# State space loop: five of ScalarE's bank reads for the linear attention taken one unit later

## The chip, the cores and the metric

The kernel runs on one core of a Trainium2 chip. The metric is the device time of one execution in microseconds. The time before is 1586.47 us, the median of three runs (1583.47 to 1590.08).

## What is computed

A decoder of two layers over 8 sequences of 256 tokens, 256 features, fp32. Layer 0 is an attention, a cross attention and a mixture of experts; layer 1 is a state space layer, a linear cross attention and a second mixture of experts. A layer norm stands behind each. The change touches the stretch in which the state space layer and the linear attention run together:

```python
# state space layer, h: 256 features x 16 states
h = exp(delta_t * A) * h + (delta_t * x_t) * B_t ;  y_t = sum_n h * C_t   # for every t
y = ys + D * x
# linear attention, context c, 16 heads of 16
K = c @ Wk.T + bk ; V = c @ Wv.T + bv ; Q = x @ Wq.T + bq
context = einsum('bhld,bhle->bhde', softmax(K, axis=tokens), V)
out = einsum('bhld,bhde->bhle', Q, context) @ Wo.T + bo
```

The context of a sequence does not depend on x. So the kernel computes for each sequence b, ahead of time, one matrix `w2[b] = Wq-part @ masked context @ Wo` and one row `lbias[b]`, and later only `x @ w2[b] + lbias[b]`.

## The kernel before

`state_space_and_linear_layers` handles the 2048 tokens in 4 chunks of 512 (two sequences each). A unit is one of the 16 states in one chunk, so there are 64 units, u = 0 to 63, with c = u // 16 and n = u % 16. Each engine runs its own loop over the units:

- VectorE (`block.vector`): in unit u, `inputs(u + 1)` (L2231, dx times the row of B in a PSUM bank), now and then a piece of the time steps (L2213, `biased`) or the attended rows (L2250, `attended`), then two scans (L2345), one for each half of the features. Each scan waits for its decay.
- ScalarE (`block.scalar`): in unit u, `decays(u + 1, 0)`, `row_of_b(u + 2)` (L2087), `decays(u + 1, 1)` (L2081), then the tasks of the unit. A decay of half h (of 128) waits until scan h - 3 is done (three banks), so `decays(u + 1, 1)` waits for the first scan of unit u. `row_of_b(u + 2)` waits until `inputs(u + 1)` is done, as there is one bank for the row.
- POOL: `h * C` (L2010) when both scans are done. TensorE: `accumulate(u - 2)` (L2410), which adds these products in PSUM, then its jobs of unit u.

The jobs are TensorE's pieces of work that go through two PSUM banks by turns (`j_banks`). The list `JOBS` numbers them: for each unit first the work for the next chunk (`AHEAD_JOBS`: T0, T1, R, D0, D1 at n = 1 to 5), then that for the chunk before (`BEHIND_JOBS`: Y0, Y1, X0, X1, Z0, Z1 at n = 2, 3, 8 to 11), then that of the linear attention (`LINEAR_JOBS`, by u % 7, a sequence every 7 units). On TensorE `start(name)` waits until the job two places before has been read out of its bank, by VectorE for D and Z, by ScalarE for all others. ScalarE reads the jobs in this order, and `j_act` counts its reads, so a waiter asks for `COUNT[name]`.

The jobs of the linear attention and ScalarE's instructions for them (`linear(job, b)` in the ScalarE block):

- u % 7 = 0: Lc (context of the sequence before, L2135) and LcT (context rows transposed, L2124)
- 1: Lk, keys: two instructions (L2127)
- 2: LM, masked context times Wo (L2138)
- 3: Lv, values (L2130), and behind it `exponentials` of the keys (L2147)
- 4: LW, combined weights (L2140)
- 5: Lb, bias row (L2142), and behind it `softmax` (L2153)
- 6: LkR, keys transposed back (L2132)

VectorE takes the maxima of the keys (L2358) at the end of its unit 7b + 2, behind the scans; it waits for ScalarE's read of Lk. The softplus (L2063, L2065) is at n = 6, the normalisations of y and z (L2092) at n = 7 and 14; TensorE's transposes X0 wait for the first.

Of the kernel before, what the change touches and what calls it, by code (L numbers as in the profile page):

```python
# [1766 lines left out]
def state_space_and_linear_layers(nc, block, sems, used_sems, x, arrivals, early, S, w, ctx_in, lw):  # L1767
# [28 lines left out]
    with ctx:  # L1796
# [66 lines left out]

        SEQS, ND = T // S, S // 128
        LINEAR_JOBS = {0: (("Lc", 1), ("LcT", 0)), 1: (("Lk", 0),), 2: (("LM", 1),), 3: (("Lv", 0),), 4: (("LW", 1),), 5: (("Lb", 1),), 6: (("LkR", 0),)}
        assert PERIOD * (SEQS + 1) < UNITS

        def linear_jobs_at(u):

            return [(job, u // PERIOD - behind) for job, behind in LINEAR_JOBS[u % PERIOD] if 0 <= u // PERIOD - behind < SEQS]  # L1870

        def sequence_at(u, n):

            return u // PERIOD if u % PERIOD == n and u // PERIOD < SEQS else None
# [165 lines left out]
        def _(act):  # L2040
# [3 lines left out]
            def taken(name):  # L2044

                act.wait_ge(j_raw, NUMBER[name] + 1)
                return bank_of(name)

            def columns(c, half):
                b = taken(f"T{half}.{c}")  # L2050
                at = c % 2 * W + half * 256
                nc.scalar.copy(xT[:, :, at:at + 256].rearrange("p k (t s) -> p t k s", t=2),
                               b.rearrange("p (t k s) -> p t k s", t=2, k=KD)).then_inc(j_act, 1)

            def projected(c):
                b = taken(f"R.{c}")
                if c >= 2:
                    act.wait_ge(bc_stored, 32 * (c - 1))
                nc.scalar.copy(rbc[:, cols(c)], b).then_inc(j_act, 1)

            def softplus(c):
                act.wait_ge(j_dve, COUNT[f"D1.{c}"])
                nc.scalar.activation(delta[:, :, cols(c)], delta[:, :, cols(c)], ACT.Exp).then_inc(dt_exp, 1)  # L2063
                act.wait_ge(dt_exp, c + 2)
                nc.scalar.activation(delta[:, :, cols(c)], delta[:, :, cols(c)], ACT.Ln, bias=one[:, 0:1]).then_inc(dt_soft, 1)  # L2065
# [7 lines left out]
            def decays(u, k):  # L2073
                c, n, half = u // N, u % N, 2 * u + k
                if u == 0:
                    act.wait_ge(dt_first, k + 1)
                elif half == 2 * N * c:
                    act.wait_ge(dt_ready, c)
                if half >= 3:
                    act.wait_ge(scanned, half - 2)  # L2080
                nc.scalar.activation(after_first(decay_ps[half % 3][:]), after_first(delta[:, k, cols(c)]), ACT.Exp,  # L2081
                                     scale=neg_a[:, k, n:n + 1]).then_inc(decayed, 1)

            def row_of_b(u):
                act.wait_ge(bc_in[u % BC_RING], 16 * (u // BC_RING) + 16)
                act.wait_ge(inp_ready, u + 1)
                nc.scalar.copy(b_ps[:], bc_rows[:, u % BC_RING, 0, :]).then_inc(b_copied, 1)  # L2087

            def normalise(c, z):
                act.wait_ge(s_shift[z], c + 1)  # L2090
                for t in range(TC):
                    last = nc.scalar.activation(x[:, c * TC + t, :], x[:, c * TC + t, :], ACT.Identity, bias=shift[z][:, t:t + 1], scale=rstd[z][:, t:t + 1])  # L2092
                last.then_inc(s_norm[z], 1)

            def normalise_arrived(n):
                act.wait_ge(m_shift, n - ON_POOL + 1)
                for t in range(arrived_parts[n].start, arrived_parts[n].stop):
                    last = nc.scalar.activation(x[:, t, :], x[:, t, :], ACT.Identity, bias=shift_m[:, t:t + 1], scale=rstd_m[:, t:t + 1])
                last.then_inc(m_norm, 1)
# [5 lines left out]
            def behind(c, job):  # L2105
                if job[0] == "Y":
                    rows_back(c, int(job[1]))
                elif job[0] == "X":
                    columns_again(c, int(job[1]))

            def total(c):
                act.wait_ge(y_total, c + 1)
                nc.scalar.copy(ysum[:, c % 2, :], y_ps[:]).then_inc(y_copied, 1)
# [6 lines left out]
            def linear(job, b):  # L2120
                p = taken(f"{job}.{b}")
                halves_of = p.rearrange("p (k s) -> p k s", k=KD)
                if job == "LcT":
                    nc.scalar.copy(cT[:], halves_of).then_inc(j_act, 1)  # L2124
                elif job == "Lk":
                    for m in range(KD):
                        last = nc.scalar.activation(kT[:, m, :], halves_of[:, m, :], ACT.Identity, bias=lbk[:, m:m + 1])  # L2127
                    last.then_inc(j_act, 1)
                elif job == "Lv":
                    nc.scalar.copy(lv[:], halves_of).then_inc(j_act, 1)  # L2130
                elif job == "LkR":
                    nc.scalar.copy(kR[:], halves_of).then_inc(j_act, 1)  # L2132
                elif job == "Lc":
                    for m in range(KD):
                        last = nc.scalar.activation(cmT[:, m, :], p[:, m * 128:m * 128 + 128], ACT.Identity, bias=lbv[:, m:m + 1])  # L2135
                    last.then_inc(j_act, 1)
                elif job == "LM":
                    nc.scalar.copy(cwo[:], halves_of).then_inc(j_act, 1)  # L2138
                elif job == "LW":
                    nc.scalar.copy(w2[:, b], halves_of).then_inc(j_act, 1)  # L2140
                else:
                    nc.scalar.copy(lbias[:, b, :], p[:, 0:D]).then_inc(j_act, 1)  # L2142

            def exponentials(b):
                act.wait_ge(k_maxed, b + 1)
                for m in range(KD):
                    last = nc.scalar.activation(kT[:, m, :], kT[:, m, :], ACT.Exp, bias=k_nmax[:, m:m + 1], accum_out=k_sums[:, m:m + 1])  # L2147
                last.then_inc(k_exped, 1)

            def softmax(b):  # L2150
                act.wait_ge(k_recip, b + 1)
                for m in range(KD):
                    last = nc.scalar.activation(kT[:, m, :], kT[:, m, :], ACT.Copy, scale=k_sums[:, m:m + 1])  # L2153
                last.then_inc(k_soft, 1)
# [14 lines left out]
            for u in range(UNITS):  # L2169
                c, n = u // N, u % N  # L2170
                if u + 1 < UNITS:
                    decays(u + 1, 0)
                    if u + 2 < UNITS:
                        row_of_b(u + 2)
                    decays(u + 1, 1)
                for m in range(ON_POOL, len(arrived_parts)):
                    if u == NORM_M_AT[m]:
                        normalise_arrived(m)
                if c + 1 < CH:
                    if n in AHEAD_JOBS and AHEAD_JOBS[n][0] == "T":  # L2180
                        columns(c + 1, int(AHEAD_JOBS[n][1]))
                    elif n in AHEAD_JOBS and AHEAD_JOBS[n] == "R":
                        projected(c + 1)
                    elif n == SOFT_AT:
                        softplus(c + 1)
                if c >= 1:
                    if n == EVAC_AT:
                        total(c - 1)
                    if n in BEHIND_JOBS:
                        behind(c - 1, BEHIND_JOBS[n])  # L2190
                    for z in "yz":
                        if n == NORM_AT[z]:
                            normalise(c - 1, z)
                for job, b in linear_jobs_at(u):
                    linear(job, b)
                if sequence_at(u, 3) is not None:
                    exponentials(sequence_at(u, 3))
                if sequence_at(u, 5) is not None:
                    softmax(sequence_at(u, 5))
# [423 lines left out]
```

## Time and profile before

| | |
|---|---|
| median of 3 runs | 1586.47 us (1583.47 to 1590.08) |
| profiled execution, its own time | 1588.36 us |
| its span, first to last instruction | 1586.6 us |
| mean granted TensorE clock | 0.933 |
| PE busy | 1384.8 us (87%) |
| VectorE (DVE) busy | 1104.2 us (70%) |
| ScalarE (ACT) busy | 934.5 us (59%) |
| POOL busy | 822.6 us (52%) |

The first scan of the loop starts at 1023.3 us and the last one ends near 1278 us. Ahead of it lie the attentions and the first mixture of experts, behind it the second one. Shares over the whole span say little about the loop. It is read from windows: the timeline of a stretch gives for each engine the start, the length, the line and, in brackets, the idle time before it and whose work ended that idle time.

### The profile page before, as it was taken

To read this page: it belongs to the slowest core of one execution; us is meant where nothing else is said; L and a number is where in the kernel's file an instruction comes from. 1 tells how busy PE (TensorE), PEld (TensorE's weight loads), DVE (VectorE), ACT (ScalarE), POOL (GpSimd) and SP (SyncE) were. 2 spreads that over 40 slices of the span, in tenths; PEclk is the share of its full clock that TensorE was granted. 3 is DMA by queue.
4 is the path that set the end of the run, shared out by engine and by line. 5 is a ranking of instruction groups with operands and counts; after the bars stand their busy time and mean duration, and the time that the engine had idled before them with its cause. 6 is when DMAs were issued, how large, how long until landed. Compare 5 with 4: busy or idle time off the path is not lost.

```text
span 1586.6 us, 27670 instructions
## 1 busy us (share of the span) xinstructions
PE 1384.8 (87%) x9268; PEld 1121.8 (71%) x9268; DVE 1104.2 (70%) x2434; ACT 934.5 (59%) x2307; POOL 822.6 (52%) x862
## 2 busy tenths in 40 slices
PE   4778999999999999956999999689899969898891
PEld 3556777777777777645999999345555549888781
DVE  5677776666666666557788874698999945656535
ACT  4666565555655655542688861377788725356553
POOL 3664554444444444433688861288868740255550
PEclk8899999999999999956999999899999987889996
DMA  4100000000000000047456668644343310244574
GB/s 150 37 28 7 28 8 8 2 8 3 6 8 2 7 2 1 1 147 272 174 202 229 233 204 298 238 133 147 124 146 135 133 60 21 94 159 162 191 250 175
DMA packets 52942, 167.85 MB, mean 106 GB/s; under 512 B 13178, under 2 KB 22340, under 8 KB 44996
## 3 DMA queue, kind: packets, MB, share of 16 engines
q1 hardware_dynamic: 45316, 145.63, 26.0%
q0 software_dynamic: 7488, 20.46, 4.0%
q8 instruction: 77, 1.26, 0.3%
q14 instruction: 61, 0.50, 0.1%
HBM read 149.28 MB, written 16.78 MB: 105 GB/s over the span
## 4 chain that ended last, share of the span: by engine, by line
PE 33%; DVE 8%; POOL 6%; issue 6%; ACT 3%; DMA 2%; POOLq 0%; DVEq 0%; ACTq 0%; SPq 0%
PE m_ps L1713 11%; PE m_ps L1736 10%; POOL s_hc L2010 4%; PE m_ps L1710 2%; DVE s_h L2345 2%; PE m_ps L1731 2%; PE m_ps L1693 1%; PE m_ps L1633 1%; PE s_yps L2410 1%; ACT s_dps L2081 1%; PE m_ps L1643 1%; PE s_yps L2497 1%; DVE tokens L1600 1%; PE m_ps L1661 1%; DMA arrived<-in_down 0%
## 5 line engine op out<-in xcount | busy, mean ns | idle before, releaser
L306 POOL TENSOR_TENSOR a_pexp<-a_pexp,a_rsum 128x384 f32<-128x384 f32 (+1 forms) x320 | 246.4, 788 | 302.6 <-DVE a_rsum L523 302.6
L396 ACT ACTIVATE a_pexp<-a_ps,a_nmax 128x384 f32<-128x384 f32 (+1 forms) x320 | 181.2, 566 | 171.7 <-DVE a_nmax L519 171.1
L1713 PE MATMUL m_ps<-m_xT,m_w1s 128*128 128x256 f32 x1344 | 213.0, 298 | 19.9 <-issue 15.3
L1736 PE MATMUL m_ps<-m_w2s,m_hs 128*128 128x256 f32 x1344 | 205.2, 290 | 4.9 <-issue 3.9
L1713 PEld LDWEIGHTS m_ps<-m_xT,m_w1s 128*128 128x128 f32 x1344 | 187.9, 203 | 23.4 <-issue 17.6
L519 DVE TENSOR_REDUCE a_nmax<-a_ps 128x1 f32<-128x384 f32 (+1 forms) x320 | 154.0, 523 | 71.1 <-PE a_ps L620 70.1
L1736 PEld LDWEIGHTS m_ps<-m_w2s,m_hs 128*128 128x128 f32 x1344 | 183.1, 197 | 6.8 <-issue 6.0
L2010 POOL TENSOR_TENSOR s_hc<-s_h,s_bc_rows 128x1024 f32<-128x1024 f32 x64 | 151.1, 2365 | 54.5 <-DVE s_h L2345 53.3
L1096 POOL DMA_INDIRECT m_xrow<-table,m_row_from x78 | 80.5, 1032 | 143.9 <-DVE m_row_from L1431 106.7
L2345 DVE TENSOR_TENSOR_SCAN s_h<-s_dps,s_inp 128x512 f32<-128x512 f32 x128 | 148.9, 1206 | 0.0
L636 PE MATMUL a_ps<-a_ident,a_pexp 128*128 128x128 f32 x896 | 144.2, 273 | 3.4 <-ACT a_pT L255 3.0
L2410 PE MATMUL s_yps<-s_hc,s_ident 128*128 128x512 f32 x256 | 124.9, 611 | 14.6 <-POOL s_hc L2010 14.2
L1113 POOL DMA_INDIRECT results<-m_yrow,m_row_to x78 | 83.5, 1071 | 75.2 <-ACT m_yrow L1225 58.8
L636 PEld LDWEIGHTS a_ps<-a_ident,a_pexp 128*128 128x128 f32 x896 | 107.3, 140 | 16.2 <-POOL a_pexp L306 5.1
L654 PE MATMUL a_ps<-a_pT,a_vx 128*64 128x256 f32 x768 | 97.0, 387 | 4.0 <-DVE a_qs_low L476 4.0
L2081 ACT ACTIVATE s_dps<-s_delta,neg_a 128x510 f32<-128x510 f32 x128 | 88.7, 693 | 12.9 <-DVE s_h L2345 12.4
L934 POOL TENSOR_TENSOR m_w2s<-arrived,m_w2s 128x512 fp32r<-128x512 f32 x60 | 79.0, 1318 | 26.6 <-ACT m_w2s L1161 26.0
L257 DVE COPY a_pT<-a_ps 128x384 f32<-128x384 f32 x128 | 70.1, 548 | 25.7 <-PE a_ps L636 25.7
L2410 PEld LDWEIGHTS s_yps<-s_hc,s_ident 128*128 128x128 f32 x256 | 47.1, 194 | 57.1 <-issue 32.7
L2231 DVE TENSOR_TENSOR s_inp<-s_dx,s_bps 128x1024 f32<-128x1024 f32 x63 | 75.9, 1204 | 11.7 <-ACT s_bps L2087 11.3
L1205 ACT ACTIVATE m_ps<-m_ps,m_b 128x256 f32<-128x256 f32 x128 | 58.4, 457 | 41.6 <-PE m_ps L1713 40.2
L1205 ACT ACTIVATE m_ps<-m_ps 128x256 f32<-128x256 f32 x96 | 35.6, 372 | 75.6 <-PE m_ps L1713 74.1
(402 smaller groups left out, 3432.4 us busy)
## 6 DMA issues: line engine op xcount, KB each, us to landing
s_bc_rows<-s_bc_table SPq DMA_DIRECT2D x64, 512.0 KB, 3.7
arrived<-in_down SPq DMA_DIRECT2D x29, 1024.0 KB, 6.5
arrived<-in_up SPq DMA_DIRECT2D x23, 1024.0 KB
m_w<-in_up SPq DMA_DIRECT2D x24, 512.0 KB
m_w<-in_down SPq DMA_DIRECT2D x24, 512.0 KB
arrived<-results SPq DMA_DIRECT2D x3, 1024.0 KB, 8.5
m_fin<-results SPq DMA_DIRECT2D x4, 768.0 KB
tokens<-in_x SPq DMA_DIRECT2D x8, 256.0 KB, 6.9
```

The costliest lines, as they stand in the source:

```text
L306: nc.gpsimd.tensor_tensor(pexp[:, r, 0:n], pexp[:, r, 0:n], rsum[:, r:r + 1].to_broadcast([128, n]), ALU.mult).then_inc(normed, 1)
L396: nc.scalar.activation(pexp[:, r, 0:n], ps_s[score_bank(u)][:, 0:n], ACT.Exp, bias=nmax[:, r:r + 1], accum_out=sums[:, r:r + 1]).then_inc( ...
L519: nc.vector.tensor_reduce(nmax[:, u % RING:u % RING + 1], ps_s[score_bank(u)][:, 0:keys_of(u)], AX.X, ALU.max, negate=True).then_inc(maxed, 1)
L636: last = nc.tensor.transpose(pt_bank(n)[:, at + k * 128:at + k * 128 + 128], pexp[:, g % RING, k * 128:k * 128 + 128], ident[:])
L654: last = nc.tensor.matmul(ps[BANK["pv", m]][64 * h:64 * h + 64, 0:S], vals[:, k, p * 128 + 64 * h:p * 128 + 64 * h + 64], pT[:, m % 2, h, ...
L1205: nc.scalar.activation(hid, hid, act, bias=b1[:, number % B_BUFS, ft:ft + 1] if b_up is not None else 0.0).then_inc(h_act, 1)
L1713: last = nc.tensor.matmul(ps_hid[ft % RING], w1s[wb][wp][:, k, of], xT[:, j % 2, xp, k, :], start=(k == 0 and wp == 0 and xp == 0), stop=( ...
L1736: last = nc.tensor.matmul(ps_y[j % 2][:, s, :], hs[hp][:, ft % RING, s * 128:(s + 1) * 128], w2s[wb][wp][:, ft, :], start=(ft == 0 and s = ...
L2010: nc.gpsimd.tensor_tensor(halves(hc[:, u % HC_RING, :]), halves(h[:, u % H_RING, :]), bc_rows[:, u % BC_RING, 1, :].unsqueeze(1).to_broadc ...
L2081: nc.scalar.activation(after_first(decay_ps[half % 3][:]), after_first(delta[:, k, cols(c)]), ACT.Exp, scale=neg_a[:, k, n:n + 1]).then_in ...
L2345: nc.vector.tensor_tensor_scan(h[:, u % H_RING, of], decay_ps[(2 * u + k) % 3][:], inp[:, u % I_RING, of], 0.0, ALU.mult, ALU.add).then_in ...
L2410: last = nc.tensor.matmul(y_ps[:, k * W:(k + 1) * W], ident[:], hc[:, u % HC_RING, k * W:(k + 1) * W], start=(n == 0), stop=False)
```

## The change

ScalarE reads the banks of five of the eight linear jobs (Lk, LM, Lv, LW, Lb) not at the end of its tasks of unit u but in unit u + 1, right behind the decays and the row of B. The order of its reads is kept, and TensorE issues all jobs where it did.

```diff
--- before.py
+++ after.py
@@ -1863,6 +1863,7 @@
 
         SEQS, ND = T // S, S // 128
         LINEAR_JOBS = {0: (("Lc", 1), ("LcT", 0)), 1: (("Lk", 0),), 2: (("LM", 1),), 3: (("Lv", 0),), 4: (("LW", 1),), 5: (("Lb", 1),), 6: (("LkR", 0),)}
+        LATE_JOBS = ("Lk", "LM", "Lv", "LW", "Lb")
         assert PERIOD * (SEQS + 1) < UNITS
 
         def linear_jobs_at(u):
@@ -2173,6 +2174,9 @@
                     if u + 2 < UNITS:
                         row_of_b(u + 2)
                     decays(u + 1, 1)
+                for job, b in linear_jobs_at(u - 1):
+                    if job in LATE_JOBS:
+                        linear(job, b)
                 for m in range(ON_POOL, len(arrived_parts)):
                     if u == NORM_M_AT[m]:
                         normalise_arrived(m)
@@ -2192,7 +2196,8 @@
                         if n == NORM_AT[z]:
                             normalise(c - 1, z)
                 for job, b in linear_jobs_at(u):
-                    linear(job, b)
+                    if job not in LATE_JOBS:
+                        linear(job, b)
                 if sequence_at(u, 3) is not None:
                     exponentials(sequence_at(u, 3))
                 if sequence_at(u, 5) is not None:
```

## Rows read from the trace of the kernel before

**Rows 1.** busy time by stretch: us, busy of each engine (x instructions), PEclk, DMA share, GB/s

```profile
1023.00:1279.00 256.00, 225.14 (x798) 136.55 (x799) 242.56 (x284) 196.76 (x379) 202.72 (x124) 0.97 0.40 134
...
1118.00:1143.00 25.00, 23.66 (x97) 16.05 (x96) 24.38 (x33) 21.28 (x43) 24.50 (x14) 1.00 0.39 129
...
1190.00:1206.00 16.00, 14.45 (x65) 10.41 (x66) 14.61 (x15) 11.63 (x23) 15.92 (x9) 1.00 0.40 136
1206.00:1279.00 73.00, 65.02 (x227) 38.25 (x226) 71.98 (x88) 55.71 (x107) 56.23 (x37) 1.00 0.32 116
```

**Rows 2.** groups of instructions, 1023 to 1279 us: busy, mean ns, idle before, releasers

```profile
L2345 DVE TENSOR_TENSOR_SCAN s_h<-s_dps,s_inp 128x512 f32<-128x512 f32 x128 | 148.9, 1206 | 0.0
...
L2231 DVE TENSOR_TENSOR s_inp<-s_dx,s_bps 128x1024 f32<-128x1024 f32 x63 | 75.9, 1204 | 11.7 <-ACT s_bps L2087 11.3
```

**Rows 3.** timeline, units 3 to 5: start us, us, engine, line, operation [idle before <-releaser]

```profile
1040.91 0.59 ACT L2130 COPY s_lv<-s_jps 128x512 f32<-128x512 f32 x1 [1.14 <-PE s_jps L2466]
...
1042.38 0.68 ACT L2081 ACTIVATE s_dps<-s_delta,neg_a 128x510 f32<-128x510 f32 x1
...
1043.60 1.22 DVE L2231 TENSOR_TENSOR s_inp<-s_dx,s_bps 128x1024 f32<-128x1024 f32 x1 [2.04 <-ACT s_bps L2087]
```

**Rows 4.** timeline, units 17 to 21

```profile
1097.96 1.22 DVE L2231 TENSOR_TENSOR s_inp<-s_dx,s_bps 128x1024 f32<-128x1024 f32 x1 [2.42 <-ACT s_bps L2087]
...
1102.87 1.22 DVE L2231 TENSOR_TENSOR s_inp<-s_dx,s_bps 128x1024 f32<-128x1024 f32 x1 [1.38 <-ACT s_bps L2087]
...
1106.82 0.37 ACT L2142 COPY s_lbias<-s_jps 128x256 f32<-128x256 f32 x1 [1.16 <-PE s_jps L2491]
...
1108.34 1.02 PE L2402 MATMUL s_jps<-s_rbc,dtw 128*128 128x512 f32 x2
...
1109.12 1.22 DVE L2231 TENSOR_TENSOR s_inp<-s_dx,s_bps 128x1024 f32<-128x1024 f32 x1 [1.07 <-ACT s_bps L2087]
...
1110.25 0.75 DVE L2213 TENSOR_SCALAR s_delta<-s_jps,dtb 128x512 f32<-128x512 f32 x1
```

**Rows 5.** timeline, a unit in VectorE's step, and the keys' pair in unit 1

```profile
1032.45 0.84 ACT L2127 ACTIVATE s_kT<-s_jps,s_lbk 128x256 f32<-128x256 f32 x2 [1.44 <-PE s_jps L2462]
...
1240.32 2.33 DVE L2345 TENSOR_TENSOR_SCAN s_h<-s_dps,s_inp 128x512 f32<-128x512 f32 x2
...
1241.57 0.69 ACT L2081 ACTIVATE s_dps<-s_delta,neg_a 128x510 f32<-128x510 f32 x1 [0.49 <-DVE s_h L2345]
```

**Rows 6.** timeline, units 22 to 32

```profile
1119.08 1.15 ACT L2065 ACTIVATE s_delta<-s_delta,s_one 128x1024 f32<-128x1024 f32 x1
...
1120.99 0.69 DVE L2358 TENSOR_REDUCE s_k_nmax<-s_kT 128x2 f32<-128x512 f32 x1
...
1122.08 1.22 DVE L2231 TENSOR_TENSOR s_inp<-s_dx,s_bps 128x1024 f32<-128x1024 f32 x1 [0.40 <-ACT s_bps L2087]
...
1154.94 1.22 DVE L2231 TENSOR_TENSOR s_inp<-s_dx,s_bps 128x1024 f32<-128x1024 f32 x1 [0.34 <-ACT s_bps L2087]
```

**Rows 7.** timeline, units 24 to 27

```profile
1125.28 1.91 PE L2466 MATMUL s_jps<-s_lwv,s_cT 128*128 128x256 f32 x8
...
1129.17 1.89 PE L2487 MATMUL s_jps<-s_cwo,s_lwq 128*128 128x256 f32 x8
...
1132.62 1.89 PE L2444 MATMUL s_jps<-s_w,s_xnT 128*128 128x256 f32 x8
...
1135.06 0.68 DVE L2250 TENSOR_TENSOR tokens<-s_jps,tokens 128x512 f32<-128x512 f32 x1
...
1137.36 1.89 PE L2444 MATMUL s_jps<-s_w,s_xnT 128*128 128x256 f32 x8
```

**Rows 8.** timeline, units 40 to 43

```profile
1191.09 0.61 PE L2489 MATMUL s_jps<-s_lbo,s_ident 128*128 128x256 f32 x2
...
1204.82 0.69 DVE L2250 TENSOR_TENSOR tokens<-s_jps,tokens 128x512 f32<-128x512 f32 x1 [0.50 <-PE s_jps L2444]
```

**Rows 9.** timeline, TensorE at the lower clock in unit 1

```profile
1028.66 3.75 PE L2462 MATMUL s_jps<-s_cT,s_lwk 128*128 128x256 f32 x8 [8.16 <-ACT s_cT L2124]
```

## The prediction

> **What bounds the kernel now.** The windows come first: between 1023 and 1279 us, where the state space loop runs its 64 units, VectorE is busy 242.56 of 256 us, TensorE 225.14, POOL 202.72 and ScalarE 196.76, so VectorE sets the pace [rows 1]. The grouped lines of that stretch say where the rest went: the scans (L2345) never had an idle moment in front of them, and the 63 products that make a unit's inputs (L2231) stood behind 11.7 us of idle, 11.3 of it until ScalarE had copied the row of B (L2087) [rows 2]. From unit 45 on (1206 to 1279 us) VectorE is busy 71.98 of 73 us. So at most some 11 us can be won here. The rest of the program keeps its order and its data; I give it nothing.
>
> Second, how near TensorE is to its own limit. It is busy 23.66 of 25 us between 1118 and 1143 (units 23 to 28) and 14.45 of 16 between 1190 and 1206 (units 40 to 43) [rows 1]. There a delay of TensorE's queue finds little room to be made up; elsewhere it does.
>
> **What moves.** No instruction is added or removed. 40 reads of a PSUM bank on ScalarE (8 each of five jobs; the keys and others are 1 or 2 instructions of 0.37 to 0.59 us) pass three ScalarE instructions: the two decays and the row of B of the next unit. No DMA and no SP or POOL instruction changes its place. The order of the jobs on ScalarE stays that of JOBS, so its counts stay true. TensorE keeps its places, and here lies the price: a job may start only when the job two before it has been read. By the job list, 14 jobs of units 17 to 51 wait for a moved read that now comes in ScalarE's turn of that same unit, behind a decay that needs VectorE's scan; before, the read came one turn earlier.
>
> **Gain at unit 5: 1.5 us.** ScalarE reads the values at 1040.91 after waiting 1.14 us for TensorE, then takes the exponentials, and starts the next decay at 1042.38; VectorE waits 2.04 us for the row behind it [rows 3]. With the read moved, wait and read (0.59, at 0.48 pitch) leave the path: 1.14 + 0.58 = 1.72 earlier. But VectorE itself comes 0.5 late from unit 2 (below) and can start its product only at 1043.60 - 2.04 + 0.5 = 1042.06: gain 1.54. Behind it VectorE has no idle until unit 19, POOL follows it, so all shifts.
>
> **Gain at units 17 to 22: 1.0 us.** Idle of 2.42, 1.38 and 1.07 us stands before three products [rows 4]. The first loses 0.7 (the value read and its wait go), the second all 1.38 (the combined weights), the third all (the bias rows' wait of 1.16 and read of 0.37). But then another wait is last: VectorE needs the first product of the time steps, TensorE's L2402 at 1108.34, done at about 1109.25, and took it at 1110.25 [rows 4]. TensorE's chain there (its products for the projection and the bias rows) isn't moved by the change. So only 1.0 us stays of some 3.5. The 0.5 of the key wait in unit 16 is swallowed here too, since the chain did not wait for VectorE.
>
> **Loss: the key maxima, 2.8 us.** L2358 on VectorE stands right behind the scans of unit 7b+2 and had never waited. Now the keys are read behind the decay that waits for the first of those scans. From a unit in VectorE's step: scans start at 1240.32 and take 2.33; the decay starts 1.25 behind their start and takes 0.69 [rows 5], so the keys' two instructions run from 1.87 to 2.71 (0.84 the pair [rows 5]). VectorE wants them at 2.25: it waits 0.5 us each time. What stands behind: the next product, all scans. Nothing else on VectorE hides it but in units 9 and 44, where statistics stand ahead of the maxima (nothing lost there). Units 2 and 16 are in the gains; units 37 and 51: 0.5 each. In unit 23 ScalarE comes from the softplus: its second half starts at 1119.08 and takes 1.15 [rows 6]; then two decays and the row (with the wait for the product) and only then the keys: from 1120.14, 0.62 + 0.50 + 0.63 between starts and 0.84 for the pair, so by 1122.7 and not 1120.9: the maxima slip from 1120.99 to 1122.75, less the idle of 0.40 that stood behind them: 1.3 [rows 6]. Unit 30, behind a normalisation of 2.1 us: 0.85, less the idle of 0.34 at 1154.94: 0.5 [rows 6]. Sum 0.5 + 0.5 + 1.3 + 0.5 = 2.8.
>
> **Loss: TensorE's queue at units 24 to 28, 1.6 us.** The values of unit 24 (1125.28 [rows 7]) need the read of LM, now behind unit 24's second decay. That waits for the first scan, which starts 1.3 late, at 1124.55; scan 1.21, decay 0.69, read 0.5: it ends at about 1127.0, so the values start 1.8 us later. Then X1, then the combined weights need the read of those values: about 1132.05 where it was 1129.17. Behind them in the queue stand an accumulation and the attended rows, 1132.62 before [rows 7] and 1135.55 then; they take 1.8. VectorE took them at 1135.06 without a wait; now at 1137.35, 2.3 late, of which 1.3 is the delay of unit 23. The second half (1137.36 on TensorE before) comes 2.9 late by the same steps. So 1.6 on top.
>
> **Loss: units 33 to 36, 0.35, and units 40 to 43, 1.45.** In unit 34 the rows going back wait for the bias rows' read (0.37 [rows 4]) and the projection behind them slips by 0.35, an estimate. In unit 40 the bias rows on TensorE (1191.09 [rows 8]) wait for the combined weights' read: 1193.15, 2 us late; X1 and the transposed keys behind it lose 1.1 to 2.2, and VectorE, which waited 0.50 for the second attended half at 1204.82 [rows 8], takes it 1.45 later.
>
> **The sum.** -1.5 - 1.0 + 2.8 + 1.6 + 0.35 + 1.45 = +3.7 us. Against the profiled execution's 1588.36 us that is 1592.1; the median of the runs shown is 1586.47, 1.9 less, so I forecast 1590.2. That is 0.23%, and this kernel's measurement can't tell less than about 0.5% (7.9 us) from no change. Bounds of what no row shows: the queue waits cost from 0 (if TensorE regains them, as it does from unit 45 on) to 1.89 us each, the eight products of one job [rows 7].
>
> **Clock.** Between 1206 and 1279 TensorE idles 8 us in small gaps and the granted clock stays 1.00, the 2.4 GHz level [rows 1]. At the lower level (1.2 GHz) the eight key products took 3.75 us (1028.66, after an idle stretch of 8.16) against 1.89 [rows 7, 9].
> The Trainium skill, TensorE: Matmul & The Clock Gate, section "A second HAM failure mode: psum-queue depth-cycling", tells of a kernel in which short idle moments between groups of matmuls, made by cycling through PSUM banks, let the clock swing between its levels. This change lengthens just such waits. The trace so far does not agree: gaps of up to 2 us left 1.00. I give it a small chance (D).
>
> **Rivals.**
> A, the forecast: gains mostly given back in other waits, +3.7, own range 1584 to 1596. Chance 0.56.
> B, the gaps close and TensorE makes up its delays: of the 11.7 us [rows 2], all but the first 0.71 (unit 0) could stand behind moved reads; at best these 11.0 go, and the key waits take 4.2 (the six, before anything is swallowed): -6.8, so 1579.7. For it: VectorE is the bound and ScalarE has 59 us to spare. Against: the gaps at 17 to 22 end in TensorE. Chance 0.24.
> C, the other side: the in-order waits of TensorE add up. In seven units (24 to 27, 37, 40, 41) a job waits for a read of the same unit; if each pushes the queue by one job of 1.89 us and the queue, over 90% busy, regains nothing: 7 x 1.89 + 4.2 - 2.5 = +14.9, 1601.4. It decides from the point at which TensorE reaches those jobs before ScalarE's second decay has ended. Chance 0.15.
> D, the clock falls in units 24 to 28 or 40 to 43: TensorE's 3 us of a unit double, three units: +9 on A, 1599. Chance 0.05.
> That the change does not do what it says is no case: the calls are plain.
>
> **From these the numbers.** Predicted 1590.2. Faster by over 0.5% (under 1578.5) is the lower third of B: 0.07. Slower by over 0.5% (over 1594.4) is 0.04 of A, 0.12 of C and 0.03 of D: 0.19. The same: 0.74. The range takes in most of B and half of C: 1579 to 1600.
>
> **What would show it.** Right: L2358 has idle of 0.4 to 1.8 us before it in six of eight cases, released by ScalarE's L2127; the idle before L2231 falls from 11.7 to some 5 us; ScalarE's waits for TensorE before L2127, L2130 and L2142 nearly vanish; TensorE's waits for ScalarE's reads appear in units 24 to 27 and 40, and VectorE waits 1 to 2 us before L2250. Wrong: L2250 unmoved (B); a wait on TensorE in every one of the same-unit cases, and then on POOL (C); a granted clock under 1.00 after 1080 us (D). It would be wrong from the ground up if VectorE's idle in the loop grew where no moved read stands.

## The result and the profile after

| | before | after |
|---|---|---|
| median of 20 runs each | 1584.66 us | 1592.57 us |
| ratio, with its 95% interval | | 1.0054 (1.0039 to 1.0068) |
| profiled execution, its own time | 1588.36 us | 1586.22 us |
| its span | 1586.6 us | 1584.5 us |
| first scan to last scan (starts) | 253.6 us | 259.1 us |
| before the first scan / behind the last one | 1023.3 / 309.7 us | 1019.5 / 305.9 us |

The kernel is slower by 8 us (the medians), 6.2 to 10.8 by the interval. The two profiled executions say the opposite by 2 us, because the stages around the loop happened to be 3.8 us shorter each in the one of after. The loop, the only place whose code changed, is 5.4 us longer.

The loop of after as a window (columns as in [rows 1]), and two short windows in it that are read further down:

```profile
1019.50:1280.90 261.40, 229.60 (x798) 138.50 (x799) 243.25 (x284) 196.84 (x379) 203.16 (x124) 0.96 0.40 131
...
1187.00:1191.00 4.00, 0.87 (x5) 0.42 (x4) 3.34 (x5) 4.00 (x8) 3.92 (x2) 1.00 0.44 153
1191.50:1195.00 3.50, 3.31 (x7) 2.52 (x8) 3.46 (x4) 3.47 (x8) 3.42 (x3) 0.52 0.05 7
```

It holds the same 284 instructions of VectorE and takes 261.4 us where it was 256 [rows 1]; the granted clock is 0.96 against 0.97. The groups of VectorE's instructions in it say where the time stands (columns as in [rows 2]):

```profile
L2350 DVE TENSOR_TENSOR_SCAN s_h<-s_dps,s_inp 128x512 f32<-128x512 f32 x128 | 148.8, 1204 | 0.0
L2236 DVE TENSOR_TENSOR s_inp<-s_dx,s_bps 128x1024 f32<-128x1024 f32 x63 | 75.8, 1203 | 7.7 <-ACT s_bps L2088 7.2
L2363 DVE TENSOR_REDUCE s_k_nmax<-s_kT 128x2 f32<-128x512 f32 x8 | 5.4, 678 | 4.1 <-ACT s_kT L2128 4.1
L2218 DVE TENSOR_SCALAR s_delta<-s_jps,dtb 128x512 f32<-128x512 f32 x7 | 5.2, 745 | 1.0 <-PE s_jps L2407 1.0
L2243 DVE BATCH_NORM_STATS2 s_stats_y<-tokens 128x6 f32<-128x256 f32 x12 | 4.2, 409 | 1.2 <-ACT tokens L2119 1.2
...
L2255 DVE TENSOR_TENSOR tokens<-s_jps,tokens 128x512 f32<-128x512 f32 x6 | 4.1, 688 | 2.8 <-PE s_jps L2449 2.8
```

The scans still never wait, and the idle before the products fell from 11.7 [rows 2] to 7.7 us: the gain. But the key maxima (L2363, L2358 before), which had never waited, stand behind 4.1 us of idle for the keys, the attended rows (L2255) behind 2.8, where it was 0.5, a statistic behind 1.2 and the time steps (L2218) behind 1.0. In all 16.8 against 12.2 us, 4.6 of the 5.4. The rest is mostly busy time: 243.25 against 242.56 us for the same 284 instructions. Without a wait an instruction of VectorE starts some 0.1 us before the one ahead has ended; behind a wait that overlap is gone.

To see where, I take from each profile the starts of the 63 products (L2231, in after L2236) from the first scan on, and subtract those of the first profile of before ("again" is a second profile of the same kernel, next section). The differences in us, at chosen units (of the inputs that are made):

| product of unit | after | after, again | before, again | moved reads behind it |
|---|---|---|---|---|
| 4 | +0.5 | +0.5 | 0.0 | key maxima of unit 2 |
| 6 | -1.6 | -1.6 | -1.3 | values of unit 3 |
| 16 | -1.2 | -1.4 | +1.7 | |
| 17 | +0.1 | -0.1 | +1.7 | |
| 23 | -1.7 | -1.9 | +0.4 | values, weights, bias rows 17 to 19 |
| 25 | -0.5 | -0.7 | +0.4 | key maxima of unit 23 |
| 30 | +1.2 | +1.0 | +0.4 | attended rows |
| 33 | +1.7 | +1.5 | +0.4 | key maxima of unit 30 |
| 39 | +2.2 | +2.0 | +2.0 | key maxima of unit 37 |
| 42 | +2.2 | +2.0 | +2.0 | |
| 45 | +4.7 | +4.5 | +2.0 | weights and bias rows of 39, 40 |
| 53 | +5.2 | +5.0 | +2.0 | key maxima of unit 51 |
| last scan | +5.4 | +5.2 | +2.0 | |

The two columns of after agree to 0.3 us. The kernel before is less steady, which the next section shows: with no edit its second profile stands at -1.3 at unit 6, so most of the gain there is one that the kernel before has in some executions too.

Two of the steps in short. The key maxima of unit 23 and what follows in TensorE's queue, the timeline of after (the values, L2471, the combined weights, L2492, the attended rows, L2449 and L2255):

```profile
1117.21 0.69 DVE L2363 TENSOR_REDUCE s_k_nmax<-s_kT 128x2 f32<-128x512 f32 x1 [1.77 <-ACT s_kT L2128]
...
1120.82 0.58 ACT L2139 COPY s_cwo<-s_jps 128x512 f32<-128x512 f32 x1
...
1121.45 1.99 PE L2471 MATMUL s_jps<-s_lwv,s_cT 128*128 128x256 f32 x8 [1.53 <-ACT s_cwo L2139]
...
1125.89 0.58 ACT L2131 COPY s_lv<-s_jps 128x512 f32<-128x512 f32 x1
...
1126.52 1.99 PE L2492 MATMUL s_jps<-s_cwo,s_lwq 128*128 128x256 f32 x8 [0.92 <-ACT s_lv L2131]
...
1130.06 1.89 PE L2449 MATMUL s_jps<-s_w,s_xnT 128*128 128x256 f32 x8
...
1131.99 0.69 DVE L2255 TENSOR_TENSOR tokens<-s_jps,tokens 128x512 f32<-128x512 f32 x1 [1.12 <-PE s_jps L2449]
```

The maxima waited 1.77 us for the keys. The values of unit 24 waited 1.53 us for ScalarE's read L2139, the weights of unit 25 waited 0.92 us for its read L2131, and VectorE then waited 1.12 us for the attended rows, before which it had no wait [rows 7].

### The profile page after: what moved, and what is told of

It reads as the page before. It is cut to its first block, busy times and chain, and to the rows that moved or that the text cites. A ratio compares the mean times of both kernels' runs of the same rounds, so it can differ in the third digit from the quotient of the medians.

```text
span 1584.5 us, 27670 instructions
## 1 busy us (share of the span) xinstructions
PE 1384.2 (87%) x9268; PEld 1117.9 (71%) x9268; DVE 1103.2 (70%) x2434; ACT 934.5 (59%) x2307; POOL 823.3 (52%) x862
## 4 chain that ended last, share of the span: by engine, by line
PE 33%; DVE 8%; issue 6%; POOL 5%; ACT 4%; DMA 2%; POOLq 0%; DVEq 0%; ACTq 0%; SPq 0%
PE m_ps L1713 10%; PE m_ps L1736 10%; POOL s_hc L2011 3%; DVE s_h L2350 2%; PE m_ps L1710 2%; PE m_ps L1731 2%; PE s_yps L2415 1%; PE m_ps L1693 1%; ACT s_dps L2082 1%; PE m_ps L1633 1%; PE m_ps L1643 1%; PE s_yps L2502 1%; DVE tokens L1600 1%; PE s_jps L2449 1%; PE m_ps L1661 1%
## 5 line engine op out<-in xcount | busy, mean ns | idle before, releaser
L1713 PE MATMUL m_ps<-m_xT,m_w1s 128*128 128x256 f32 x1344 | 208.7, 294 | 17.6 <-issue 15.3
L1713 PEld LDWEIGHTS m_ps<-m_xT,m_w1s 128*128 128x128 f32 x1344 | 183.4, 198 | 21.4 <-issue 17.4
L2236 DVE TENSOR_TENSOR s_inp<-s_dx,s_bps 128x1024 f32<-128x1024 f32 x63 | 75.8, 1203 | 7.7 <-ACT s_bps L2088 7.2
```

What stands on the lines that cost most here:

```text
L1713: last = nc.tensor.matmul(ps_hid[ft % RING], w1s[wb][wp][:, k, of], xT[:, j % 2, xp, k, :], start=(k == 0 and wp == 0 and xp == 0), stop=( ...
```

## The experiments

The theory, W in the expectations, is that of the first section: the loss is waits inside the loop, for the keys and in TensorE's queue, and low clock. Its rivals are that the low clock is chance (P), that part of the loss lies outside the loop (O), that VectorE's wait only replaces a later one (S) and that low clock costs nothing (N). Each run is told with its ratio to the kernel before on the same chip, and with its loop, first to last scan. The loop is that of one profile. The runs are from three chips. On one of them (the next four runs) the whole program took some 30 us less, all of it behind the loop (272 to 276 us from the last scan to the end there, 303 to 314 elsewhere), so loops and ratios are compared and not times.

### The two kernels once more

No edit.

> The changed kernel once more, for a second profile. Theory W (the waits: key maxima 4.1 us, attended rows 2 us, the low clock in units 14 and 40 about 3 us, less the gaps that closed): the same idle before the key maxima, 6 of 8, 4.0 to 4.3 us, and a distance from the first to the last scan of 257 to 260 us against 253.6 before. Rival P (the two stretches of low clock fell there by chance of phase and belong to no cause of the change): the maxima wait as much, but the low clock stands in other units or in none, and the distance is near 256. Rival O (a part of the 8 us lies outside the loop): time 1.003 to 1.007 of the kernel before with a loop only 2 to 5 us longer.

> The kernel before once more, for a second profile. W: first to last scan 253 to 255 us, no low clock after unit 10. P: low clock at 1.2 GHz somewhere behind unit 10 here too, with a distance of 255 to 257. Ratio 1.000, within 0.2%.

The changed kernel: 1.0038 (1.0024 to 1.0052), loop 258.8 us, the maxima wait 4.1 us in six units again. The kernel before: 0.9995 (0.998 to 1.0009), loop 255.6 us: 2.0 us longer than in its first profile. It gained 1.3 us by unit 6, lost 3.0 by the product of unit 13, got 1.3 of that back in the gap of unit 20, and lost 1.7 between units 33 and 36. At unit 13 TensorE's clock was at its lower level, 1.2 GHz (a window of before, again, with the columns of [rows 1]: PEclk is the one behind POOL's):

```profile
1062.00:1066.00 4.00, 3.71 (x5) 1.65 (x6) 4.00 (x4) 1.66 (x3) 3.21 (x3) 0.50 0.43 154
```

The values of unit 10 took 3.14 us for what the next job did in 1.89 (timeline of the same run):

```profile
1065.86 3.14 PE L2466 MATMUL s_jps<-s_lwv,s_cT 128*128 128x256 f32 x8
...
1070.56 1.89 PE L2487 MATMUL s_jps<-s_cwo,s_lwq 128*128 128x256 f32 x8
```

The first profile of before has such a stretch too, in TensorE's units 7 and 8, behind an idle moment of 1.93 us (a line of its timeline and a window):

```profile
1054.19 1.26 PE L2478 MATMUL s_jps<-s_kR,s_lv 128*128 128x128 f32 x8 [1.93 <-ACT s_kR L2132]
...
1055.10:1058.40 3.30, 3.30 (x10) 2.00 (x9) 3.28 (x4) 3.27 (x8) 3.22 (x3) 0.50 0.41 159
```

It cost nothing: the kernel before with filled unit 1 (below) has no low clock there and the same distances between the products from unit 6 to 16.

So a loop of the kernel before is 253.6 or 255.6 us, by where stretches of low clock fall; rival P is right for this kernel. In the changed kernel both profiles have them in the same two places, units 14 and 40; the run with products of zeros, below, takes them apart. Rival O does not fall: on this chip the time is 5.9 us longer (3.7 to 8.1) and the loop 3.1 us longer than that of before, again.

### The key maxima

```diff
             for u in range(UNITS):
                 c, n = u // N, u % N
                 if u >= 1 and u + 1 < UNITS:
                     inputs(u + 1)
+                b = sequence_at(u, 3)
+                if b is not None:
+                    dve.wait_ge(j_act, COUNT[f"Lk.{b}"])
+                    nc.vector.tensor_reduce(k_nmax[:], kT[:], AX.X, ALU.max, negate=True).then_inc(k_maxed, 1)
...
-                b = sequence_at(u, 2)
-                if b is not None:
-                    dve.wait_ge(j_act, COUNT[f"Lk.{b}"])
-                    nc.vector.tensor_reduce(k_nmax[:], kT[:], AX.X, ALU.max, negate=True).then_inc(k_maxed, 1)
```

> The changed kernel with VectorE's key maxima moved behind the next product (unit 7b+3), so that they never wait; all five reads stay late. W: idle before the maxima 0; the loop is 3.5 to 4.5 us shorter than that of the changed kernel, ratio to the kernel before 1.001 to 1.004. Rival S (VectorE's wait only takes the place of a later one, since ScalarE and TensorE hold it up anyway): the loop is less than 1.5 us shorter and the idle before the products grows instead.

Ratio 1.0007 (0.9993 to 1.0021), loop 257.3 us. The groups of VectorE:

```profile
L2236 DVE TENSOR_TENSOR s_inp<-s_dx,s_bps 128x1024 f32<-128x1024 f32 x63 | 75.6, 1201 | 10.2 <-ACT s_bps L2088 9.8
...
L2339 DVE TENSOR_REDUCE s_k_nmax<-s_kT 128x2 f32<-128x512 f32 x8 | 5.4, 677 | 0.2 <-ACT s_kT L2128 0.2
```

The 4.1 us before the maxima are gone but for 0.2. At the product of unit 42 this loop stands at -0.2 against the first profile of before, where the changed kernel stands at +2.2: without its maxima's wait the change costs nothing up to there. Then it lost 3.5 us from unit 43 to 45, where after lost 2.4, and the idle before the products is 10.2: the low clock in unit 40 was longer here (from 1192.3 to 1199.0 us, in after from 1191.5 to 1195.0). So the 1.8 us that the loop as a whole gained understate the key wait; up to unit 42 the gain is 2.4. W's 3.5 to 4.5 us for the loop were missed, and so was its ratio, by a little.

The same from the other side, the keys at their old place:

```diff
-        LATE_JOBS = ("Lk", "LM", "Lv", "LW", "Lb")
+        LATE_JOBS = ("LM", "Lv", "LW", "Lb",)
```

> The changed kernel with the keys read at their old place (LM, Lv, LW, Lb stay late). W: no idle before the maxima, 3 to 4 us less than the changed kernel, but ScalarE waits for TensorE before the keys as it did before (some 11 us) and VectorE's idle before its products is 1 us larger than with the maxima moved. Ratio 1.002 to 1.004. Rival S: within 1.5 us of the changed kernel.

Ratio 1.0018 (1.0000 to 1.0036), loop 254.3 us, 4.8 less than after, where W had 3 to 4; no idle before the maxima, -0.5 at unit 42. Of the 4.8 us, 2.7 are gained by unit 42, 1.6 are the low clock of unit 40, which is absent here, and 0.5 the maxima of unit 51. ScalarE waits 9.1 us before the keys (W: some 11), and VectorE's idle before its products is 7.3 us, less than the 10.2 with the maxima moved and not more, since that run had the longer low clock. And the keys alone:

```diff
-        LATE_JOBS = ("Lk", "LM", "Lv", "LW", "Lb")
+        LATE_JOBS = ("Lk",)
```

> Only the keys (Lk) are read one unit later, the four others at their old place. W: the price of the key maxima alone: idle before them in 5 or 6 of 8 units, 3.5 to 4.3 us, first to last scan 256.5 to 258.5 us (254.6 is the mean of the two profiles of the kernel before), TensorE without a new wait behind it, ratio 1.001 to 1.004. Rival S: the maxima wait but the loop is within 1 us of the kernel before, because gaps before the products close instead.

Ratio 1.0019 (1.0001 to 1.0036), loop 255.9 us:

```profile
L2236 DVE TENSOR_TENSOR s_inp<-s_dx,s_bps 128x1024 f32<-128x1024 f32 x63 | 75.7, 1202 | 9.7 <-ACT s_bps L2088 9.5
...
L2363 DVE TENSOR_REDUCE s_k_nmax<-s_kT 128x2 f32<-128x512 f32 x8 | 5.4, 678 | 4.1 <-ACT s_kT L2128 4.1
```

The same 4.1 us as with all five. The loop is 2.3 us over the first profile of before, 0.6 under W's range, since gaps behind take part of each wait: the steps are +0.5 (unit 4), swallowed at unit 6; +0.5 (18), swallowed at 20; +1.2 (25), +0.4 (30 to 33), +0.5 (39), +0.5 (53). All are where the prediction had them.

### Values alone, weights and bias rows alone

```diff
-        LATE_JOBS = ("Lk", "LM", "Lv", "LW", "Lb")
+        LATE_JOBS = ("Lv",)
```

> Only the values (Lv) are read one unit later. Theory V (the late values in unit 24 hold up the combined weights of unit 25 and so the attended rows): the gap before the product of unit 6 closes (2 us gained there), 0.5 to 1.5 us gained at unit 20, and VectorE falls back by 1.5 to 1.8 us between units 28 and 30, waiting before the attended rows. Rival: no fall between units 28 and 30, the queue takes the delay up, as it did with only weights and bias rows late.

```diff
-        LATE_JOBS = ("Lk", "LM", "Lv", "LW", "Lb")
+        LATE_JOBS = ("LW", "Lb",)
```

> Only the combined weights and the bias rows (LW, Lb) are read one unit later. Theory Q (TensorE's wait for the late weights in units 26 and 40 is what delays the attended rows): the wait of 1.5 us before the bias rows in unit 40 is there, the attended rows wait, the gaps before the products of units 21 and 22 close; loop 253 to 256 us. If the low clock follows from that wait it stands in unit 40 here too (3 us more); if it is chance it may be absent. Rival: without the late values the weights run 2.9 us earlier in unit 25 and the attended rows of units 27 and 28 do not wait.

Values alone: 0.9995 (0.997 to 1.002), loop 254.0. Gained 2.1 at unit 6. Of the 1.5 us gained at unit 20, 1.3 only take back what low clock had cost at unit 17. Lost 1.7 from unit 27 (-1.3) to unit 29 (+0.4). The timeline there, in the terms of [rows 7]:

```profile
1131.77 1.99 PE L2492 MATMUL s_jps<-s_cwo,s_lwq 128*128 128x256 f32 x8 [1.46 <-ACT s_lv L2131]
...
1135.31 1.89 PE L2449 MATMUL s_jps<-s_w,s_xnT 128*128 128x256 f32 x8
...
1137.24 0.69 DVE L2255 TENSOR_TENSOR tokens<-s_jps,tokens 128x512 f32<-128x512 f32 x1 [0.50 <-PE s_jps L2449]
```

The weights wait 1.46 us for ScalarE's late read of the values, and the attended rows come late for VectorE. Weights and bias rows alone: 1.0007 (0.9983 to 1.0032), loop 255.0, of which low clock took 1.4 between units 33 and 36; from unit 27 to unit 30 it stands at -0.9 (unit 29: -1.1). So theory V holds: it is the late values that delay the attended rows of units 27 and 28, and the queue does not take the delay up. Theory Q is right for unit 40 and for the gaps of units 21 and 22 (-1.5 at unit 21): this run lost 0.9 us from unit 42 to 45 (+0.3 to +1.2). Its wait before the bias rows in unit 40 is 1.50 us, as in after, with the clock there at its full level.

### The clock in units 14 and 40

The changed kernel in unit 40. TensorE's X0 (L2441) waits for the normalised rows, the bias rows (L2494, L2496) for the late read of the weights (L2141):

```profile
1189.56 0.63 PE L2441 MATMUL s_jps<-s_ident,tokens 128*128 128x128 f32 x4 [2.32 <-ACT tokens L2093]
...
1191.06 0.58 ACT L2141 COPY s_w<-s_jps 128x512 f32<-128x512 f32 x1
...
1191.69 1.22 PE L2494 MATMUL s_jps<-s_lbo,s_ident 128*128 128x256 f32 x2 [1.50 <-ACT s_w L2141]
...
1192.70 1.91 PE L2496 MATMUL s_jps<-s_cwo,s_lbq 128*128 128x256 f32 x4
...
1194.41 2.12 PE L2415 MATMUL s_yps<-s_hc,s_ident 128*128 128x512 f32 x4
...
1199.20 1.22 DVE L2236 TENSOR_TENSOR s_inp<-s_dx,s_bps 128x1024 f32<-128x1024 f32 x1 [1.70 <-ACT s_bps L2088]
```

The bias rows take 1.22 and 1.91 us. In the kernel before, X0 waits 1.32 us there and the bias rows not at all, so the change lengthened the idle moments of this unit. But in the keys-in-place run the same three took 0.63, 0.70 and 1.03, behind gaps of 1.80 and 1.50 us:

```profile
1189.61 0.63 PE L2441 MATMUL s_jps<-s_ident,tokens 128*128 128x128 f32 x4 [1.80 <-ACT tokens L2093]
...
1191.74 0.70 PE L2494 MATMUL s_jps<-s_lbo,s_ident 128*128 128x256 f32 x2 [1.50 <-ACT s_w L2141]
...
1192.27 1.03 PE L2496 MATMUL s_jps<-s_cwo,s_lbq 128*128 128x256 f32 x4
```

```profile
1191.50:1195.00 3.50, 3.26 (x12) 2.10 (x13) 3.46 (x4) 3.48 (x8) 3.42 (x3) 1.00 0.03 5
```

The window of 3.5 us shows 1.00 there and 0.52 in after (first section): the levels of 2.4 and 1.2 GHz, half of the clock in nearly all of that window. From 1187 to 1191 us, just ahead of it, TensorE was busy for 0.87 us in after (first section) and for 1.44 in the keys-in-place run. The run with the maxima moved had the gaps of the keys-in-place run (1.80 and 1.50 us) and the low clock of after. So the length of the gaps does not settle it.

In unit 14 the change lengthened nothing. The accumulation there waits 2.0 us for POOL with and without the change. One line each of before, of after, and of the kernel before with filled unit 1 (below):

```profile
1079.24 1.98 PE L2410 MATMUL s_yps<-s_hc,s_ident 128*128 128x512 f32 x4 [2.02 <-POOL s_hc L2010]
...
1074.32 2.74 PE L2415 MATMUL s_yps<-s_hc,s_ident 128*128 128x512 f32 x4 [2.01 <-POOL s_hc L2011]
...
1077.43 2.55 PE L2412 MATMUL s_yps<-s_hc,s_ident 128*128 128x512 f32 x4 [2.01 <-POOL s_hc L2012]
```

The first ran at the full clock. Behind the other two the clock fell, and the third has no late read at all. So that a late read makes the low clock of unit 14 is not shown. To take the low clock away without moving another instruction (the cleared tile `zero` and the counts for it are left out here):

```diff
+            def add_zeros(count, start=False):
+                for n in range(count):
+                    nc.tensor.matmul(y_ps[:, 0:W], zero[:, 0:1].to_broadcast([128, 128]), lwo[:].rearrange("p k d -> p (k d)"), start=start, stop=start)
...
+                add_zeros({14: 1}.get(u, 0))
                 if u >= LAG:
                     accumulate(u - LAG)
+                add_zeros({40: 1}.get(u, 0))
...
+                add_zeros({40: 1}.get(u, 0), u == 1)
                 for job, b in linear_jobs_at(u):
                     linear(job, b)
```

> The changed kernel with one product of zeros of 0.86 us added to the sum in PSUM in each of three idle stretches of TensorE: ahead of the accumulation of unit 14 (idle 2.0 before), ahead of X0 and ahead of the bias rows in unit 40 (idle 2.3 and 1.5). No other instruction is moved. Theory C (the stretches of low clock behind these gaps cost about 1.3 us at unit 17 and 1.5 to 2 us at units 44 and 45): the low clock is gone from both, the loop is 255 to 256.5 us against 258.9. Rival N (the low clock costs nothing there, the queue waits alone do): 258 to 260 us.

Ratio 1.0024 (1.0003 to 1.0045), loop 256.7 us. TensorE in unit 40 (L2508 are the added products):

```profile
1190.18 1.02 PE L2508 MATMUL s_yps<-s_lwo,s_zero 128*128 128x512 f32 x2
...
1192.66 0.63 PE L2443 MATMUL s_jps<-s_ident,tokens 128*128 128x128 f32 x4 [1.46 <-ACT tokens L2095]
...
1193.12 1.02 PE L2508 MATMUL s_yps<-s_lwo,s_zero 128*128 128x512 f32 x2
...
1194.79 0.70 PE L2496 MATMUL s_jps<-s_lbo,s_ident 128*128 128x256 f32 x2 [0.64 <-ACT s_w L2143]
...
1195.32 1.03 PE L2498 MATMUL s_jps<-s_cwo,s_lbq 128*128 128x256 f32 x4
```

The gaps that remain are 1.46 and 0.64 us, and L2496 and L2498 take 0.70 and 1.03. At unit 17 the loop stands at -1.4 (after: +0.1) and it loses 0.9 us from unit 42 to 45 (after: 2.5). So 2.3 of the 5.4 us of the loop are low clock in two places, and 3.1 are waits. C's mechanism holds, its range ended 0.2 below the measured loop; N falls. These 5.4 us count from the first profile of before, to which its low clock behind unit 6 cost nothing. In its second profile it did, as told above, and the loop of after is only 3.4 us longer than that one.

### A version with less to lose

Late reads only where a gap stands behind them:

```diff
-        LATE_JOBS = ("Lk", "LM", "Lv", "LW", "Lb")
+        LATE_JOBS = ("Lv", "LW", "Lb")
+        LATE_UNITS = (3, 17, 18, 19)
...
-                    if job in LATE_JOBS:
+                    if job in LATE_JOBS and u - 1 in LATE_UNITS:
...
-                    if job not in LATE_JOBS:
+                    if job not in LATE_JOBS or u not in LATE_UNITS:
```

> Only the reads of units 3, 17, 18 and 19 are late (the values of units 3 and 17, the weights of 18, the bias rows of 19); all other reads and the key maxima as before. W: the gaps of 2.0, 2.4, 1.4 and 1.1 us before the products shrink to some 1 us in all and nothing is lost behind: 2.0 to 2.8 us less than the kernel before, loop 250.8 to 253 us where no low clock falls into units 10 to 60. Rival S: less than 1 us less, since the next wait (first time steps in unit 21) takes it back.

Loop 251.9 us, at -3.4 from unit 23 to unit 33, then 1.7 lost to low clock by unit 36. The product's idle is 8.0 us:

```profile
L2237 DVE TENSOR_TENSOR s_inp<-s_dx,s_bps 128x1024 f32<-128x1024 f32 x63 | 75.8, 1203 | 8.0 <-ACT s_bps L2089 7.6
```

The loop is 1.7 us shorter than the first profile of before and 3.8 shorter than the second, where W had 2.0 to 2.8; without the low clock, at unit 33, it was 3.4 ahead of the first. The whole kernel is at 0.9994 (0.9976 to 1.0011), which is no difference that these runs can tell.

With the same products of zeros: `add_zeros({1: 8}.get(u, 0), u == 1)` ahead of the linear jobs, in the idle stretch of 8.2 us [rows 9], first in the kernel before, then with the four reads; and last with one more in each of the units 7, 14, 31 (ahead of the accumulation), 24 and 40 (behind it).

> The kernel before with eight products of zeros on TensorE (0.86 us each at 2.4 GHz) ahead of the keys of unit 1, in an idle stretch of 8.2 us. Theory C: the low clock of units 1 to 4 goes, and with it part of the gap of 2.0 us before the product of unit 6; loop 251.5 to 253 us. Rival N: the loop stays at 253.6 to 255.6 us.

> The four late reads (units 3, 17, 18, 19) and the eight products of zeros in unit 1. If both gains add: 2.5 to 4 us less than the kernel before, loop 250 to 252 us; if the late read of unit 3 and the clock close the same gap of unit 6, no more than with the four reads alone (251.9).

> The four late reads, the eight products of zeros in unit 1 and one more in units 7, 14, 31, 24 and 40 each, in gaps of 1.3 to 2.0 us of TensorE. C: no low clock between units 2 and 60, where single profiles of the kernel before had 1 to 3 such stretches: loop 249.5 to 251.5 us, ratio 0.997 to 0.999. Rival: the added products come late where a gap is short, and the loop is no shorter than with the fill in unit 1 alone.

The kernel before, filled: 0.9982 (0.996 to 1.0004), loop 253.8. It closed the gap of unit 6 whole (-2.1 at the product, where the low clock had been), but low clock stood later in the loop, as in the second profile of before: it cost 1.2 us at unit 17, half of which the gap of unit 20 took back, and 1.7 between units 33 and 36. The expectation of 251.5 to 253 was missed by that. The four reads, filled in unit 1: 0.9979 (0.9955 to 1.0003), loop 252.0: no more than without the fill, since both close the same gap of unit 6 (-2.1 in either), and again low clock, 3.0 us at unit 13. All fills: loop 250.2 us, the granted clock at 0.99 over the loop (window, columns as in [rows 1]):

```profile
1022.00:1275.00 253.00, 231.16 (x820) 137.44 (x819) 243.37 (x285) 196.60 (x380) 202.26 (x124) 0.99 0.41 137
```

It is the shortest loop of all, 3.4 and 5.5 us under the two of the kernel before; the whole kernel is at 0.9988 (0.9964 to 1.0012). No version is clear of the noise; the four reads with all fills is the best candidate by the loop (by the ratio it is the one with the fill in unit 1 alone), and that it beats the kernel before as a whole is not shown.

## Why the prediction held, step by step

The forecast was +3.7 us, to 1590.2; measured are +8 (6.2 to 10.8) and 1592.57, and in the second measurement, on another chip, 1.0038, 5.9 us (3.7 to 8.1). The time lies in the range and the sign is right; the size is the open part. The range, 1579 to 1600, took in no change and a small gain as well, so to lie in it says little. The waits in the loop were forecast well (3.7, measured 3.1). The loop came to 5.4 with low clock, and the whole to 8, and what goes beyond the waits comes from no term of the sum.

| term | forecast | in the profiles of after | |
|---|---|---|---|
| gain at unit 5 | -1.5 | -1.1 | -1.6 at the product, 0.5 given back at the next piece, which waited for the time steps |
| gain at units 17 to 22, with unit 16's maxima | -1.0 | -1.1 | unit 16 to 23 in the run without low clock (-1.4 to -2.5); the waits that end it are 1.17 us before a statistic, which the forecast does not name, and 0.60 before the time steps, which it does |
| key maxima, units 23, 30, 37, 51 | +2.8 | +2.7 | 1.25 + 0.43 + 0.5 + 0.5; the idle in front of all six is 4.1 |
| attended rows, units 24 to 28 | +1.6 | +1.7 | units 28 to 30 |
| units 33 to 36 | +0.35 | +0.1 | 33 to 37 |
| units 40 to 43 | +1.45 | +0.9 | 42 to 45 in the run without low clock |
| low clock, unit 14 | 0 | +0.6 | 1.3 at unit 17, of which the gap at unit 20 takes 0.7: 16 to 23 is -0.5 in after |
| low clock, unit 40 | 0 | +1.6 | 42 to 45, 2.5 less 0.9 |
| sum | +3.7 | +5.4 | the loop's +5.4; steps of 0.2 or less (units 7 to 16, unit 58) are left out |

Point by point:

- That VectorE bounds the loop and its only idle is before the products held; in the loop the sum of waits in front of VectorE moved as the loop did, from 12.2 to 16.8 us.
- The step that failed is the one on the clock. From the long stretch with small gaps at 1.00 [rows 1] I drew that gaps of up to 2 us are harmless, and gave rival D 0.05. But TensorE's largest gap there is 1.00 us, but for 3.08 and 1.37 us before its last two accumulations at the very end, and the same trace has 0.50 behind the gap of 1.93 at 1054.19 us, which I overlooked. The sum put the clock at nothing, and in after it cost 2.3 us in two places by the filled run, less than the 9 that D had as a case of its own. Only one of the two, unit 40, has D's mechanism, waits that the change lengthened (from 1.32 and none to 2.32 and 1.50 us); and two runs with the weights late and the clock at its full level there (keys in place; weights and bias rows alone) show that such waits need not bring it. The kernel before loses 3.0 and 1.7 us to low clock in its second profile, so whether the change adds to it on average stays open.
- The rule of the Trainium skill that I weighed (TensorE: Matmul & The Clock Gate, "A second HAM failure mode: psum-queue depth-cycling"), that waits between groups make the clock swing, was the better guide than the row. The trace of after agrees in unit 40, with 0.52 in the window behind the waits of 2.32 and 1.50 us; behind waits of 1.80 and 1.50 us two runs differ, one with 1.00 and one with the low level.
- Rival B, that TensorE makes its delays up, fell: the attended rows waited 2.8 us, and with the values alone late the loss was the same 1.7 us. Rival C, each wait of the same unit paid in full, fell too: of seven, two groups cost something, 1.7 and 0.9 us, not 13. The 4.2 us that B and C give the key waits count unit 23 after its gap has taken a part (1.3); by the same working the six waits are 4.6, and 4.1 were measured.
- What I named as the signs: the maxima's idle in six of eight (shown, 0.4 to 1.77 us), the products' idle down to some 5 us (7.7 with low clock, 5.6 in the filled run), ScalarE's waits before the keys, the values and the bias rows gone (11.1, 3.5 and 4.0 us before, none in after), TensorE's waits for late reads in units 24, 25 and 40 (1.53, 0.92, 1.50), VectorE waiting 1 to 2 us before the attended rows (1.12 and 0.69, and about 0.5 each in units 43 and 44). The sign against it that I gave for D, a granted clock under 1.00 after 1080 us, came true as well.
- Open: the loop explains 5.4 us (against the first profile of before; 3.4 against the second), the timing says 6.2 or more in the first measurement and 3.7 or more in the second, where the two loops differ by 3.1. So some 3 to 5 us of the 8 may lie in executions with a longer loop than the profiled ones or outside the loop (rival O). From the last scan to the end the ten profiles on the other chips take 303 to 314 us, with no order by kernel (before 309.7, after 305.9, the four late reads 314.0), so a part outside the loop is neither shown nor ruled out. How often low clock falls into the loop of either kernel over many runs, which would move the mean, was not measured.

## What to carry to other kernels

When a read on an in-order engine is put behind a wait, look for two things: who stands at the reading engine's pace on the other side (here the maxima, 2.7 us), and which job two places on needs the bank (here 1.7 and 0.9). Take the late place only where a gap stands behind the read: four of the forty reads gave the loop 3.4 us by unit 23, where all forty gave 2.5 at best. And take a second profile before a small cost is put down to a change: the same kernel's loop differed by 2.0 us between two profiles.

## What the runs showed of the hardware

Low clock is not settled by the gaps that one sees just ahead of it. Behind gaps of 1.80 and 1.50 us TensorE ran at full clock in one kernel (three instructions of 0.63, 0.70 and 1.03 us) and at half in another with the same two gaps; with 0.86 us of added work in each gap it stayed at full clock. A stretch at half clock behind unit 6 cost the loop 0 to 3.0 us, by where it fell: nothing in units 7 and 8, 1.2 to 1.3 us at the product of unit 17, 1.7 between units 33 and 36, 3.0 at unit 13. And filling one idle stretch of 8.2 us did not end it: with the fill in unit 1 alone the kernel before had it at units 17 and 36, with all six places filled the loop had it nowhere in its one profile.
